# One core, decoder layer: the fills of TensorE in the delta-net stage laid out anew over the six inverse levels

## The reference

```python
qkv = x @ W_qkv.T ; z = x @ W_z.T                 # 16 key heads, 2 value heads each, 128 wide
qkv = causal_conv4(qkv) ; k = k / max(|k|, 1e-12)
def step(state, (q_t, k_t, v_t, b_t, d_t)):       # over 256 tokens, 8 sequences
    delta = (v_t - k_t @ state) * b_t
    state = state * d_t + outer(k_t, delta)
    o = q_t @ state
out = rmsnorm(o) * norm_w * silu(z)
y = out.reshape(B, T, -1) @ W_out.T
```

## Time and profile before

| | |
|---|---|
| time, median of 3 runs (lowest, highest) | 4244.57 us (4244.35, 4247.62) |
| time of the profiled execution | 4249.73 us |
| its span, first to last instruction | 4247.9 us |
| PE, DVE, ACT, POOL busy, share of the span | 92%, 69%, 57%, 15% |
| mean granted TensorE clock | 0.967 |
| delta stage, about | 126 us to 2890 us |

### The profile page before, as it was taken

The page is one execution under the profiler, slowest core; times in us unless marked ns, Lnnn a source line. Parts: engine busy times, 40 slices in busy tenths (PEclk is TensorE's granted clock), DMA queues, the critical chain, the costliest instruction groups (busy, mean ns, idle before and its releaser), DMA issues. The chain is left out here.

```text
span 4247.9 us, 69123 instructions
## 1 busy us (share of the span) xinstructions
PE 3922.7 (92%) x26288; PEld 2918.6 (69%) x26288; DVE 2951.4 (69%) x5022; ACT 2426.1 (57%) x4813; POOL 638.1 (15%) x585
## 2 busy tenths in 40 slices
PE   3899999999999999999999999995798989699998
PEld 2677777777777777777777777773444444488886
DVE  3788888888888888888888888874555556322222
ACT  2677777777777767777776777662444445311111
POOL 0000000000000000000000000002356555310110
PEclk7999999999999999999999999997899999899999
DMA  2010111010100101011000111003656574310001
GB/s 77 16 43 26 33 36 33 26 34 25 38 31 26 43 16 43 26 33 36 29 30 30 29 36 33 26 16 64 108 97 112 101 118 86 94 33 8 21 16 40
DMA packets 156674, 188.05 MB, mean 44 GB/s; under 512 B 13340, under 2 KB 97052, under 8 KB 156348
## 3 DMA queue, kind: packets, MB, share of 16 engines
q1 hardware_dynamic: 153916, 182.62, 18.1%
q10 hardware_dynamic: 2432, 1.05, 0.2%
HBM read 151.31 MB, written 30.15 MB: 43 GB/s over the span
## 5 line engine op out<-in xcount | busy, mean ns | idle before, releaser
L406 PE MATMUL pj<-xh,w_hi 128*128 128x512 f32 x1536 | 684.5, 446 | 16.8 <-DVE w_lo L745 16.6
L406 PE MATMUL pj<-xh,w_lo 128*128 128x512 f32 x1536 | 607.5, 396 | 0.0
L406 PE MATMUL pj<-xl,w_hi 128*128 128x512 f32 x1536 | 600.9, 391 | 0.0
L1054 POOL TENSOR_TENSOR silu_z<-silu_z,exp_z 128x512 f32<-128x512 f32 x128 | 191.8, 1521 | 2602.7 <-ACT exp_z L632 2602.7
L1607 DVE TENSOR_REDUCE row_max<-s 128x1 f32<-128x512 f32 x512 | 341.0, 686 | 277.3 <-PE s L1353 274.2
L1539 ACT ACTIVATE probs<-s 128x512 f32<-128x512 f32 x512 | 293.5, 594 | 319.6 <-PE s L1377 315.5
L406 PEld LDWEIGHTS pj<-xh,w_hi 128*128 128x128 f32 x1536 | 291.2, 190 | 65.5 <-DVE w_lo L745 17.0
L406 PEld LDWEIGHTS pj<-xh,w_lo 128*128 128x128 f32 x1536 | 288.9, 188 | 66.2
L406 PEld LDWEIGHTS pj<-xl,w_hi 128*128 128x128 f32 x1536 | 292.3, 190 | 50.0 <-issue 14.8
L1377 PE MATMUL s<-q_stack,k_stack 128*128 128x512 f32 x512 | 252.3, 495 | 72.0 <-DMA q_stack<-row_maxima 66.2
L811 DVE SCALAR_TENSOR_TENSOR conv_v<-conv_in,conv_w_section,conv_v 128x512 f32<-128x512 f32 x384 | 287.9, 750 | 10.7 <-ACT conv_v L615 1.6
(11 more groups left out here) (257 smaller groups left out, 9937.7 us busy)
## 6 DMA issues: line engine op xcount, KB each, us to landing
w_raw<-in_w_in SPq DMA_DIRECT2D x128, 256.0 KB, 6.4
decays<-decay_by_head SPq DMA_DIRECT2D x64, 512.0 KB, 3.7
decays<-decay_by_head SPq DMA_DIRECT2D x64, 256.0 KB, 5.5
q_stack<-qk_parts SPq DMA_DIRECT2D x128, 128.0 KB
k_stack<-qk_parts SPq DMA_DIRECT2D x128, 128.0 KB
f_raw<-in_f_w SPq DMA_DIRECT2D x32, 256.0 KB, 2.7
x_all<-in_x SPq DMA_DIRECT2D x4, 1024.0 KB, 10.8
source<-in_ctx SPq DMA_DIRECT2D x8, 512.0 KB
```

What stands on the lines that cost most here:

```text
L406: mm = pe.matmul(pj[j % 2][:, :], a[:, j, k * P:(k + 1) * P], b[:, k, bp * WIN:(bp + 1) * WIN], start=(n == 0), stop=(n == 3 * KT - 1))
L1054: pool.tensor_tensor(sz[p][:, :], sz[p][:, :], ez[p][:, :], ALU.mult).then_inc(E["sz"].sem, 1)
```

## The change

Only the order of PE's list is changed. The DVE, ACT, POOL and SP lists are the same, row for row. `pe_project` and `pe_y` take a range of products, `lo` to `hi`, instead of a half or a whole. The waits stand ahead of the first product of a bank, the event behind its last. `pe_section` fills by `fill(lv, side)`:

| gap | before | now |
|---|---|---|
| (1, 0) to (2, 1) | 6 each | 6 each |
| (3, 0), (3, 1) | 6, 6 of `VALUE + 1` | 6, 5 of `VALUE + 1` |
| (4, 0) | 6 of output tile 0 | the last of `VALUE + 1`, 6 of tile 0 |
| (4, 1) | 6 of tile 1 | 4 of tile 1 |
| (5, 0) | 6 of tile 2 | 2 of tile 1, 2 of tile 2 |
| (5, 1) | 6 of tile 3 | 4 of tile 2 |
| (6, 0) | none | 6 of tile 3 |
| (6, 1) | none | `pe_norms` |
| `d0p` to `rp` | `pe_norms` | 4 of `GATE` |
| `rp` to `dp2` | 6 of `GATE` | 4 of `GATE` |
| `dp2` to `cp` | 6 of `GATE` | 4 of `GATE` |

```diff
-        def pe_project(pe, t, bp, j, hk_w, s, half):
+        def pe_project(pe, t, bp, j, hk_w, s, lo, hi):
...
-            n = 2 * 3 * half
-            for k in (2 * half, 2 * half + 1):
-                for a, b in ((w_hi, xh), (w_hi, xl), (w_lo, xh)):
-                    mm = pe.matmul(pj[j % 2][:, :], a[:, j, k * P:(k + 1) * P],
-                                   b[:, k, bp * WIN:(bp + 1) * WIN], start=(n == 0), stop=(n == 3 * KT - 1))
-                    n += 1
-            if half == 1:
+            for n in range(lo, hi):
+                k = n // 3
+                a, b = ((w_hi, xh), (w_hi, xl), (w_lo, xh))[n % 3]
+                mm = pe.matmul(pj[j % 2][:, :], a[:, j, k * P:(k + 1) * P],
+                               b[:, k, bp * WIN:(bp + 1) * WIN], start=(n == 0), stop=(n == 3 * KT - 1))
+            if hi == 3 * KT:
                 mm.then_inc(E["pj" if j < GATE else "pz"].sem, 1)
...
+            def out(i, lo, hi):
+                if prev:
+                    pe_y(pe, s + -1, prev[0], i, ("c3", s + 1, VALUE) if nxt else ("vc", s, 0), lo, hi)
+
+            def fill(lv, side):
+
+                if lv in (1, 2):
+                    proj(lv, side)
+                elif lv == 3:
+                    proj(VALUE + 1, lo=6 * side, hi=6 + 5 * side)
+                elif (lv, side) == (4, 0):
+                    proj(VALUE + 1, lo=11)
+                    out(0, 0, 6)
+                elif (lv, side) == (4, 1):
+                    out(1, 0, 4)
+                elif (lv, side) == (5, 0):
+                    out(1, 4, 6)
+                    out(2, 0, 2)
+                elif (lv, side) == (5, 1):
+                    out(2, 2, 6)
+                elif (lv, side) == (6, 0):
+                    out(3, 0, 6)
+                elif nxt:
+                    pe_norms(pe, s + 1)
...
             for lv in range(1, LEVELS):
-                a, b = gap.get(lv, (lambda: None,) * 2)
                 pe_x(pe, s, lv, 0, prev)
                 pe_x(pe, s, lv, 1, prev)
-                a()
+                fill(lv, 0)
                 pe_tu(pe, s, lv, 0)
                 pe_tu(pe, s, lv, 1)
-                b()
+                fill(lv, 1)
 
             E["uc"].wait(pe, s, 0)
             E["vr"].wait(pe, s, 0)
             pe_group(pe, xp[0], lambda q: u_f[:, 0, mat(q)], v_r, "d0p")
-            if nxt:
-                pe_norms(pe, s + 1)
+            proj(GATE, lo=0, hi=4)
             E["d0"].wait(pe, s, 0)
             pe_group(pe, xp[1], lambda q: a_t[:, q, 0:P], d0[:, :].bitcast(F32), "rp")
-            proj(GATE, 0)
+            proj(GATE, lo=4, hi=8)
             E["res"].wait(pe, s, 0)
             pe_group(pe, tp, lambda q: u_f[:, 0, mat(q)], res, "dp2")
-            proj(GATE, 1)
+            proj(GATE, lo=8)
```

More of the change, by code:

```diff
@@ L386, in half_pair @@
                            ap=[list(at.ap[0]), [W + b, 2], [2 * b, H // b], [1, b]])
-        def pe_project(pe, t, bp, j, hk_w, s, half):
-            if half == 0:
+        def pe_project(pe, t, bp, j, hk_w, s, lo, hi):
+            if lo == 0:
                 if bp == 0:
@@ L447, in pe_out_norms, with pe_y @@
             pe.matmul(sum_bank[p][:, :], ones, osq[p][:, :], start=True, stop=True).then_inc(E["oss"].sem, 1)
-        def pe_y(pe, s, hk, i, bank_read):
-            if i == 0:
+        def pe_y(pe, s, hk, i, bank_read, lo=0, hi=3 * PV):
+            if i == 0 and lo == 0:
                 E["ghi"].wait(pe, s, 1)
@@ L454, in pe_y @@
                 w_split.wait(pe, hk, PIECES - 1)
[L455 to L465, removed]
+            if lo == 0:
+                if i < 2:
+                    E[bank_read[0]].wait(pe, bank_read[1], bank_read[2] + i)
+                else:
+                    E["yadd"].wait(pe, s, i - 2)
+            for n in range(lo, hi):
+                p = n // 3
+                a, b = ((g_hi, wo_hi), (g_hi, wo_lo), (g_lo, wo_hi))[n % 3]
+                mm = pe.matmul(pj[i % 2][:, :], a[p][:, i * P:(i + 1) * P], b[:, p, :], start=(n == 0),
+                               stop=(n == 3 * PV - 1))
+            if hi == 3 * PV:
+                mm.then_inc(E["y"].sem, 1)
         def pe_first(pe, s, c, after_out):
@@ L513, in pe_section, with proj @@
         def pe_section(pe, s, bp, hk, prev, nxt, first, more):
-            def proj(j, half):
+            def proj(j, half=None, lo=0, hi=3 * KT):
+                if half is not None:
+                    lo, hi = 3 * KT // 2 * half, 3 * KT // 2 * (half + 1)
                 if j >= GATE:
-                    pe_project(pe, s, bp, j, hk, s, half)
+                    pe_project(pe, s, bp, j, hk, s, lo, hi)
                 elif nxt:
-                    pe_project(pe, s + 1, nxt[1], j, nxt[0], s, half)
+                    pe_project(pe, s + 1, nxt[1], j, nxt[0], s, lo, hi)
+            def out(i, lo, hi):
[20 more added lines that the diff above has]
+                    pe_norms(pe, s + 1)
             pe_values(pe, s, 0)
@@ L587, in pe_prologue @@
             for j in range(GATE):
-                for half in range(2):
-                    pe_project(pe, first, 0, j, 0, None, half)
+                pe_project(pe, first, 0, j, 0, None, 0, 3 * KT)
             pe_norms(pe, first)
```

## The result

The changed kernel takes 4265.04 us (4259.38 to 4268.93, 6 runs) against 4245.97 us (4244.35 to 4250.61, 6 runs) of the kernel before: ratio 1.0043, 95% interval 1.003 to 1.0056. It is 19 us slower. Its profiled span is 4263.3 us, against 4247.9.

What follows compares the result with a forecast made beforehand. PE's list was taken to set the period, with gains only where PE waits. Window terms 0.72 + 0.06 + 0.77 + 0.06 = 1.61 us a head, 26 us in 16 heads, gave 4244.6 + 26 = 4270, range 4257 to 4283.

Steps and rivals of the forecast that it cites:

- the main case: Whole kernel: new waits at `cp` and level 5 outweigh the level 6 gain; 4270, 4257 to 4283, 62 in 100.
- The solve, d0p to cp: PE reaches `cp` at 4.76 us after `d0p` starts but waits 0.67 for DVE's `delta`, possible only at 5.43.
- Level 5, window 0: ACT's weights fix the start of `pe_tu`'s second half; 2.97 us follow, level 6 +0.50, section +0.72.
- Level 5, window 2: ACT bounds; `x_l` comes 0.34 us later, `pe_tu` of level 6 +0.55, section +0.77.
- Level 5, windows 1 and 3: PE waits 0.30 us for `x_l` behind `v_tok` rounding; level 6 starts -0.16, section +0.06, window 1 counted the same.
- Sections: The four windows of a head were to take about 43.7, 44.1, 44.1 and 42.6 us.
- From level 6 to cp: `pe_tu` of level 6 to `cp`: 0.54 + 0.91 + 5.43 = 6.88 us against 6.66, +0.22 in every section.
- Price of a fill: First product behind a small f16 group takes 0.32 us, the next 0.23; an added fill costs 0.09 extra.
- Rival 2: The chain to `cp` is shorter than read, level-5 waits stay; 0.67 falls away in 64 sections: 4228, 7 in 100.
- Rivals 1 and 3: 1: nothing new waits, 4183, 4 in 100; 3: level-5 waits don't come, `cp`'s does, 4232 to 4251, 13 in 100.
- Rival 4: Fills of four also miss level-4 and level-5 copies, by 0.2 to 0.4 us a section: 4283 to 4296, 14 in 100.

Runs made afterwards that it cites:

- solve_only: The kernel before with only the change's solve part: (6, 0) empty, `pe_norms` in (6, 1), gate projection in three parts; 4260.32 us, ratio 1.003.
- norm_early: The changed kernel with DVE's norm guard moved ahead of the solve's `v_tok`, and ACT's Ln and Exp ahead of the beta copies; 4226.67 us, ratio 0.9947.
- weights_late: The changed kernel with ACT's rounding of two weight pieces in windows 0 and 2 moved from level 4 to level 6; 4233.62 us, ratio 0.9964.
- both_round: The changed kernel with early norm readers, weight pieces of windows 0 and 2 late, and ACT's rounding of `v_tok` at level 3; 4181.48 us, ratio 0.9841.
- before_late: The kernel before, fills untouched, with the weight pieces of windows 0 and 2 moved to level 6; 4281.05 us, ratio 1.0072.

## Why the prediction was right, and where it was off

The forecast was 4270, 26 us over before; 19 were measured, and the main case held.

- *The solve, d0p to cp.* Right. A wait of 0.67 at `cp` in every section was forecast, 0.58 is there, and 0.57 in `solve_only`. Its cause, the place of guard, Ln and Exp, is shown by `norm_early`: it goes when only they are moved.
- *Level 5, window 0.* Right. From the second half of `pe_tu` of level 5 to `pe_tu` of level 6, it takes 1540.26 - 1537.28 = 2.98 us; the sum had 2.97, and before it was 2.47. That the weights ahead of `x_l` hold it is shown by `weights_late`.
- *Level 5, window 2.* Right. The second half was to start 0.34 later and `pe_tu` of level 6 0.55 later; they start 0.33 later (1625.25 - 1601.86 = 23.39, against 1617.47 - 1594.41 = 23.06) and 0.55 later (1628.23 - 1601.86 = 26.37, against 1620.23 - 1594.41 = 25.82).
- *Level 5, windows 1 and 3.* A wait of 0.30 was forecast. In window 3 it is 0.27, and its cause, the rounding of `v_tok`, is shown by `both_round`, where it is 0.02. Window 1 was counted like window 3, at +0.06, and came out at -0.07: its wait is only 1581.17 - 1580.87 - 0.12 = 0.18.
- *Sections.* 43.7, 44.1, 44.1 and 42.6 forecast, 43.56, 43.93, 44.06 and 42.58 measured.
- *From level 6 to cp.* This is the term that was mis-sized: forecast 6.88, measured 1677.50 - 1670.80 = 6.70. Two parts of it are seen. The halves of `pe_tu` follow at 0.24 and 0.22, not at the 0.27 that stood in the earlier trace rows: that 0.27 had held a wait for the second copy, so I had priced a wait as work. And the norm with `d0p` behind it takes 1.31 (1671.26 to 1672.57), not 0.91 + 0.50. In the terms of the sum: `pe_tu` 0.46 for 0.54, the norm up to `d0p` 0.63 for 0.91, and `d0p` to `cp` 5.61 for 5.43. Together 0.18 us a section, 11 us too much. Against it stands 0.10 that the sum did not have: `cp` takes 0.99 behind a wait, and took 0.89 behind a product, by the timeline of the kernel before:

```profile
1669.45 1.05 PE L509 MATMUL up<-v_tok,a_t 128*128 128x128 f32 x8
1670.34 0.60 PE L427 MATMUL ms<-k_normed 128*128 128x256 f32 x2
```

  The difference, 0.08 in 64 sections, is 5 of the 7 us. The rest lies within the spread of the runs. The number came close because the mechanism was right; it isn't luck.
- *Price of a fill.* Behind `pe_x` of level 5 in window 0 of the changed kernel the first product takes 1535.02 - 1534.70 = 0.32, as in the earlier trace rows. Its weight load starts only 0.03 ahead of it, that of the product behind it 1535.02 - 1534.79 = 0.23 ahead:

```profile
1534.67 0.19 PEld L462 LDWEIGHTS pj<-wo_lo,u_final 128*128 128x128 f32 x1
1534.79 0.19 PEld L462 LDWEIGHTS pj<-wo_hi,residual 128*128 128x128 f32 x1
```

  The rule of the Trainium skill ("TensorE: Matmul & The Clock Gate", Part 2), by which loads are pulled ahead of products in flight and the added fill would cost no extra, is seen from one wide product to the next, and isn't borne out for the first product behind the small f16 group, the one that the prediction priced.
- *Rivals.* Rival 2, a shorter chain, needed an order of ACT and DVE that the change did not have; `norm_early` made that order, and gave the 41 us that the rival put at 43. Rivals 1 and 3 are out by the waits of 0.58 at `cp` and of 0.80 and 0.27 at level 5. Rival 4, more waits at levels 4 and 5, would have made windows 1 and 3 longer, and they moved by -0.07 and +0.01.

## What to carry to other kernels

When an operation is moved to an earlier gap of one engine, its readers have to be looked up in the lists of the other engines: here the norm went from behind `d0p` to ahead of it and was still read behind `d0p`'s copies, and two moved calls turned a loss of 19 us into a gain of 22. A fill is not free work: it covers whatever the other engines do at that point, so taking two products out of each of two gaps shows at once in the windows where ACT had weights to round. Where fills and the work that they cover can both be moved, the moves are worth trying together. In this kernel the late weights alone cost 31 us and the new fills alone 8; together, with the new solve and its early readers, they win 54.

## What the runs showed of the hardware that I had not expected

In `before_late` most sections of window 0 take 43.56 us, but six of them 45.1, and two of window 2 take 46.0 where the rest take 44.4. One of the first kind starts at 998.89. PE from `d0p` on, and the windows behind it:

```profile
1025.97 0.66 PE L509 MATMUL xp<-rhs_rounded,u_final 128*128 128x128 f32 x4 [1.40 <-ACT u_final L698]
1026.47 1.50 PE L416 MATMUL ms<-square,ones 128*128 128x512 f32 x2
1027.76 1.91 PE L509 MATMUL xp<-delta_first,a_t 128*128 128x128 f32 x8
1029.33 0.77 PE L406 MATMUL pj<-xh,w_hi 128*128 128x512 f32 x1
```

```profile
1027.19:1030.69 3.50, 3.50 (x13) 2.97 (x13) 2.29 (x4) 2.59 (x7) 0.00 (x0) 0.54 0.00 0
1030.69:1034.89 4.20, 4.20 (x27) 3.75 (x26) 2.61 (x4) 1.56 (x4) 0.00 (x0) 1.00 0.00 0
```

The granted clock stands at 0.54 in the first window, nearly all of it at the lower of its two levels, 1.2 GHz, and is back at 1.00 in the next; the same matmul group takes 1.57 us from start to start where it took 0.85 in the other sections of this run. Ahead of it PE had waited 0.36 at level 6 and then 1.40 for `u_final`. The loss is about 1.6 us a time, 8 x 1.6 = 13 us. With the 24 us of longer waits that makes the 37 us by which the delta stage of this execution is longer than before (2757.7 from the first section's start to the last's, against 2720.8). The execution took 4285.01, 4 above the median of 4281.05. The others fit: the two with a mean granted clock of 0.967 took 4275.06 and 4276.57, the one with 0.966 took 4281.05, and the other with 0.965 took 4288.86. No section of the kernel before or of the changed kernel is longer than its kind, though in windows 0 and 2 of the changed kernel PE waits about 1 us at level 5. All 30 sections of `before_late` in which ACT rounds the weights late have that same wait of 1.40, and in 22 of them the clock stays up; what picks the eight is not shown. The Trainium skill, "TensorE: Matmul & The Clock Gate", section "A second HAM failure mode: psum-queue depth-cycling", describes another kernel, in which short idle times between groups of matmuls, coming often, make the clock go down and up again; this run agrees in so far as two or three short waits stand ahead of each fall. So where the clock fell, a wait of 1.4 us on PE cost about twice its length.
